# Selective scan of a two-layer conditioned network: new slot tables for the work laid around the scan, and SiLU work regrouped

## The chip, the core and the metric

One Trainium2 chip, one of its cores. The metric is device time of one launch in microseconds (us). A core has a matrix engine (TensorE, PE in the profile; its weight loads are PEld), VectorE (DVE), ScalarE (ACT), GpSimd (POOL) and SyncE (SP), which only issues transfers here. Each runs its own instruction stream in program order, and they wait for one another by semaphores.

## The reference, cut to what matters

Eight samples of 512 tokens by 512 features pass through a conditioned linear-attention layer, then through a layer with softmax attention and a selective scan. The change touches the scan and what follows it:

```python
# xm: layer-normed, scaled and shifted x, (b, 512, 512); DI = 1024, N = 16, K = 4
xr, z = split(xm @ W_in, 2)
u = silu(causal_conv(xr, W_conv, K) + b_conv)          # per channel, 4 taps
dt, Bm, Cm = split(u @ W_x, [64, 80])
delta = softplus(dt @ W_dt + b_dt)
A = -exp(A_log)
h = exp(delta_t * A) * h + (delta_t * u_t) * B_t       # for each t, 1024 x 16 states
y = sum(h * C_t) + u * D_param
ssm = (y * silu(z)) @ W_out
full = silu(ln(concat(ssm, attention)) @ W_full + b_full)
out = x + gate * full
```

Everything is float32.

## The kernel before

A setup block and a block with both attentions for all samples come first and are not touched. The last block, `mix` (L873), does the scan layer, and all that follows is about it.

**Units and slots.** A sample b is done in two halves (channels 0 to 511, then 512 to 1023); a half is 16 states times two groups of 256 channels, so 32 units. Each engine's stream has one step, called a slot, for each unit, and 32 slots make a half. In slot s

- ACT writes the decays exp(delta*A) of unit s+2 into one of two PSUM pairs (`decay`, L1187, two instructions). It must wait until the unit two before it is scanned (L1184);
- POOL writes delta*u*B of unit s+4 into one of six buffers (`dbu`, L1110), after PE has turned what lay in that buffer (L1105);
- DVE scans unit s+2 (L1342, one instruction over two times 512 steps) and then, from slot 2 on, adds two token tiles of y to `acc` (L1347, called the adds here);
- PE transposes two token tiles of a scanned state into `y_bank` (`turn`, L1480, eight matmuls, called the turn). Its two banks come free with DVE's adds of the slot before.

At slot 0 the half before is closed: PE turns `acc` back (`total`, L1489), DVE adds u*D and multiplies with silu(z) (L1356, L1360, L1367). Then PE turns four tiles of state 0, and ACT begins the new sum with them at its slot 1 (`set_sum`, L1218).

**Work laid into the slots.** After its scan work each engine does in a slot what dictionaries name for that slot (L925 to L960): `PE_XR = {0: 0, 1: 1, 3: 2, ...}` means that PE computes product xr2 in slot 3. Two streams of such work are laid beside a sample's scan:

- `front(n, s)`, beside half 1 of sample n-1: the products xr0 to xr7 (each four float32 matmuls, eight instructions in the profile, L1463), their convolution (first tap on ACT, `ACT_CONV0`, L1245, three taps on DVE, `DVE_CONV`, L1379), SiLU of u (`ACT_SILU_U`), the products z0 to z7, the projection xd, dt and C. Then softplus of channels 0 to 511: five ACT instructions for each 128 channels (`ACT_A1`), a pair of logarithms between two table loads (`ACT_LN1`), and four instructions on POOL (`POOL_CORR1`, `POOL_DELTA1`; L1116, L1119, L1125, L1128). The other four dt are done beside half 0 of sample n itself (`PE_DT0`, `ACT_A0`, `ACT_LN0`, `POOL_CORR0`, `POOL_DELTA0`).
- `tail(p, s)`, beside half 0 of sample p+1 and the first slots of its half 1 (counted on as slots 32, 33, ...): for each of four token tiles t the output product (`PE_O`, two slots), its copy (`ACT_O`), layer norm (`DVE_STATS`, `ACT_LN`, `DVE_NEWTON`, `ACT_NORM`), two transposes (`PE_CT`), their copies (`ACT_CT`), the last product (`PE_F`, two slots), the bias (`DVE_F`, L1416), SiLU (`ACT_OUT`), gate and residual on POOL (`POOL_OUT`, L1141, L1144) and the store (`SP_STORE`).

In half 1 PE does `front(n, 0)`, which holds xr0, ahead of slot 0's `total`. The first sample's `front` runs alone before the first scan, and the last sample's `tail` alone after the last.

**The ring.** All these products share two PSUM banks in program order (`Ring`, L73, and `order`, L976): a use waits until the use two before it was emptied (`wait_free`, L94), by ACT or DVE as named in `front_uses` and `tail_uses`. If the emptying sits in slot s+1 of ACT and the new use in slot s of PE, PE waits for an instruction that stands one slot later.

**ACT's tables.** SiLU is in another table set than the exponential. Each group of SiLU on ACT is led by an ACT_TABLE_LOAD and followed by one that brings the exponential back (`preload_act_table_set`). A sample has nine such groups: two for u, four for z (L1223, L1224) and three for the output (L1289, L1290). The logarithms of softplus add four groups.

**SyncE** issues the rows of B ahead of POOL (`load_row`, four rows, which are eight slots, ahead), the weights (`weights`, L1022: W_in, W_out and W_full take turns in two places), the attention tiles, x1 tiles, the gate and the stores, in its own slots.

Of the kernel before, what the change touches and what calls it, by code (L numbers as in the profile page):

```python
# [872 lines left out]
def mix(nc, a, out, space, bank, ident, col, aneg, convw, x1_d, xm_d, attn_d, gate_d, b_d, wide, load_wide, arrived):  # L873
    ctx = ExitStack()
    with ctx:
# [126 lines left out]
        with nc.Block() as block:  # L1002
# [174 lines left out]
            def _(act):  # L1177
# [48 lines left out]
                def front(n, s):  # L1226
                    if s in ACT_UD and n:
                        for c in ACT_UD[s]:
                            if n >= 2:
                                act.wait_ge(ring.full, ring.at(n - 2, "f3"))  # L1230
# [394 lines left out]
```

## Time and profile before

| | us |
|---|---|
| median of 3 runs (4289.5 to 4292.44) | 4291.6 |
| the profiled execution: its time | 4291.85 |
| the profiled execution: its span | 4290.1 |
| setup and attention, up to the `mix` block | about 1805 |
| `mix` | about 2485 |
| one sample in the middle of `mix` (two halves) | 296.97 |

In the timeline an instruction is printed with its start, its length, and in brackets how long its engine had been idle before it and which instruction ended that idle time. Neighbouring instructions of the same kind are merged (x2). The samples of `mix` repeat one another closely, so the sample that starts at 2757.93 (b = 3, whose half 1 starts at 2902.63) is read for all. A slot is counted from the start of its scan on DVE.

### The profile page before, as it was taken

The page shows a single profiled execution, that of the slowest core. Times are in us where ns is not written, and L with a number is a line of the kernel's source. Part 1 is how long each engine was busy: PE and PEld are TensorE (multiplying, and loading weights), DVE is VectorE, ACT ScalarE, POOL GpSimd, SP SyncE. Part 2 cuts the span into 40 slices and gives each one's busy share as a digit, 9 for nine tenths or more (in the row PEclk, how much of TensorE's full clock was granted, in tenths as well). Part 3 has the DMA queues.
Part 4 walks back from the last instruction along what each step waited for, and adds up shares of the span by engine and source line. Part 5 has one row for each costly group of instructions (what it writes and reads, how often), then busy time and mean ns, then how long its engine had stood idle before and what let it go on. Part 6 is the DMA issues. An engine that isn't in the chain of part 4 may idle for free.

```text
span 4290.1 us, 36188 instructions
## 1 busy us (share of the span) xinstructions
PE 3455.3 (81%) x12298; PEld 1819.9 (42%) x12298; DVE 2852.3 (66%) x3658; ACT 1991.9 (46%) x3326; POOL 1901.0 (44%) x1139
## 2 busy tenths in 40 slices
PE   5798989898898988676877787778787778878857
PEld 1444444343444443234444444444444444444444
DVE  1344445353535352349998888898889989888993
ACT  0232323232223231165666665675766657656743
POOL 0021212121212121147675775774766766757761
PEclk8899999999999999885888888889788888888858
DMA  5001010101010101011112222112121121122110
GB/s 201 32 1 42 0 42 1 42 1 42 1 42 1 42 1 69 29 33 35 60 66 81 71 78 85 62 66 80 64 79 65 64 79 64 69 87 71 43 51 20
DMA packets 99798, 220.85 MB, mean 51 GB/s; under 512 B 10576, under 2 KB 10688, under 8 KB 97568
## 3 DMA queue, kind: packets, MB, share of 16 engines
q1 hardware_dynamic: 95904, 211.06, 14.6%
q10 hardware_dynamic: 3712, 7.47, 0.5%
q8 instruction: 100, 1.64, 0.2%
q14 instruction: 82, 0.67, 0.0%
HBM read 184.67 MB, written 33.83 MB: 51 GB/s over the span
## 4 chain that ended last, share of the span: by engine, by line
PE 16%; DVE 16%; issue 9%; POOL 9%; ACT 7%; DMA 0%; POOLq 0%; SPq 0%; DVEq 0%
PE bank L1463 12%; DVE HS L1342 7%; DVE acc L1347 6%; POOL HS L1110 5%; PE bank L1480 4%; ACT bank L1187 2%; ACT G L1283 1%; POOL delta L1125 1%; POOL ZS L1116 1%; POOL DU L1128 1%; DVE U L1379 1%; PE bank L1489 1%; DVE G L1367 0%; ACT L1224 0%; DVE stats L1401 0%
## 5 line engine op out<-in xcount | busy, mean ns | idle before, releaser
L1110 POOL TENSOR_TENSOR HS<-DU,brep 128x1024 f32<-128x1024 f32 x512 | 1196.4, 2355 | 693.2 <-PE bank L1480 693.2
L1342 DVE TENSOR_TENSOR_SCAN HS<-bank,HS 128x1024 f32<-128x1024 f32 x512 | 1167.1, 2280 | 79.6 <-ACT bank L1187 59.4
L1480 PE MATMUL bank<-ident,HS 128*128 128x128 f32 x4096 | 697.8, 322 | 385.5 <-DVE acc L1347 351.0
L1187 ACT ACTIVATE bank<-delta,aneg 128x511 f32<-128x511 f32 x1024 | 662.9, 681 | 537.8 <-DVE HS L1342 536.2
L1480 PEld LDWEIGHTS bank<-ident,HS 128*128 128x128 f32 x4096 | 563.5, 165 | 660.1 <-DVE HS L1342 426.8
L1347 DVE SCALAR_TENSOR_TENSOR acc<-bank,C,acc 128x512 f32<-128x512 f32 x960 | 668.3, 737 | 146.0 <-PE bank L1480 144.9
L431 POOL TENSOR_TENSOR PR<-PR,rrec 128x512 f32<-128x512 f32 x256 | 261.3, 1042 | 895.2 <-DVE rrec L665 895.2
L1463 PE MATMUL bank<-w_l,G 128*128 128x512 f32 x1024 | 528.1, 666 | 42.2 <-ACT G L1283 40.2
L1463 PE MATMUL bank<-XM,w_l 128*128 128x512 f32 x1024 | 512.8, 649 | 30.3 <-ACT delta L1197 14.3
L520 ACT ACTIVATE PR<-bank,nsmax 128x512 f32<-128x512 f32 x256 | 173.5, 682 | 449.5 <-DVE nsmax L661 449.4
L715 PE MATMUL bank<-w_l,NT 128*128 128x512 f32 x768 | 358.5, 612 | 0.9 <-ACT NT L487 0.9
L1463 PEld LDWEIGHTS bank<-w_l,G 128*128 128x128 f32 x1024 | 213.1, 219 | 277.2 <-issue 232.1
L1463 PEld LDWEIGHTS bank<-XM,w_l 128*128 128x128 f32 x1024 | 207.2, 212 | 262.9 <-issue 222.7
L661 DVE TENSOR_REDUCE nsmax<-bank 128x1 f32<-128x512 f32 x256 | 164.7, 685 | 191.6 <-PE bank L815 191.6
L822 PE MATMUL bank<-ident,PR 128*128 128x128 f32 x1024 | 172.2, 294 | 134.5 <-DVE PT L672 121.4
L672 DVE COPY PT<-bank 128x512 f32<-128x512 f32 x256 | 175.4, 685 | 95.7 <-PE bank L822 95.7
L822 PEld LDWEIGHTS bank<-ident,PR 128*128 128x128 f32 x1024 | 121.6, 148 | 265.5 <-issue 225.8
L715 PE MATMUL bank<-XM,w_l 128*128 128x512 f32 x512 | 223.5, 597 | 6.8 <-issue 6.8
L715 PEld LDWEIGHTS bank<-w_l,NT 128*128 128x128 f32 x768 | 143.9, 197 | 171.1 <-issue 147.1
L1379 DVE SCALAR_TENSOR_TENSOR U<-bank,convw,U 128x509 f32<-128x509 f32 (+2 forms) x192 | 143.3, 747 | 52.7 <-ACT U L1245 48.2
L815 PE MATMUL bank<-K,Q 64*128 64x512 f32 x512 | 146.7, 650 | 9.4 <-ACT K L510 6.2
L715 PEld LDWEIGHTS bank<-XM,w_l 128*128 128x128 f32 x512 | 97.3, 191 | 132.5 <-issue 132.5
(164 smaller groups left out, 3817.8 us busy)
## 6 DMA issues: line engine op xcount, KB each, us to landing
brep<-b_d SPq DMA_DIRECT2D x256, 256.0 KB, 3.2
w_l<-in_L_cond_W_in SPq DMA_DIRECT2D x14, 2048.0 KB, 9.8
w_l<-in_L_cond_W_out SPq DMA_DIRECT2D x7, 2048.0 KB, 8.5
...
```

The lines of the kernel that those rows point to most:

```text
L431: nc.gpsimd.tensor_tensor(p, p, rrec[:, hp % 2, t, e:e + 1].to_broadcast([P, T]), ALU.mult).then_inc(pnorm, 1)
L520: nc.scalar.activation(PR[:, hp % 2, e, t, :], sc_bank[e][:], ACT.Exp, bias=nsmax[:, hp % 2, t, e:e + 1], accum_out=rsum[:, hp % 2, t, e:e ...
L672: nc.vector.tensor_copy(PT[:, k % 2, e, :], pt_bank[:]).then_inc(pt_done, 1)
L715: last = nc.tensor.matmul(dst[:], lhs(c), rhs(c), start=(c == 0), stop=(c == DC - 1))
L822: last = nc.tensor.transpose(pt_bank[:, t * P:(t + 1) * P], PR[:, hp % 2, e, t, k * P:(k + 1) * P], ident[:])
L1110: nc.gpsimd.tensor_tensor(HS[:, u % DEEP], DU[:, chunks(j, s), :], brep[:, m % 3, :].unsqueeze(1).to_broadcast([P, UC, T]), ALU.mult).then ...
L1187: last = nc.scalar.activation(dA[:, s, i, 1:T], delta[:, c, 1:T], ACT.Exp, scale=aneg[:, c, n:n + 1])
L1342: nc.vector.tensor_tensor_scan(h, dA[:, u % 2].rearrange("p i t -> p (i t)"), h, 0.0, ALU.mult, ALU.add).then_inc(scanned, 1)
L1347: nc.vector.scalar_tensor_tensor(out=acc[:, t, :], in0=y_bank[t % 2][:], scalar=C[:, j // 2 % 2, t, n:n + 1], in1=acc[:, t, :], op0=ALU.mu ...
L1379: last = nc.vector.scalar_tensor_tensor(out=y, in0=ring.bank(n, f"xr{c}")[:, 0:T - lag], scalar=convw[:, c, k:k + 1], in1=y, op0=ALU.mult, ...
L1463: last = nc.tensor.matmul(dst, lhs(c), rhs(c), start=(c == 0), stop=(c == of - 1))
L1480: last = nc.tensor.transpose(y_bank[t % 2][:, i * P:(i + 1) * P], h, ident[:])
```

## The change

It replaces the slot tables of `mix` and moves three pieces of ACT's work. Nothing is computed otherwise, and no instruction is added except through the order; ACT_TABLE_LOADs fall away.

- The eight xr products go from pairs (0, 1, 3, 4, 6, 7, 9, 10) to threes (0, 1, 2, 4, 5, 6, 8, 9), with the convolutions, z, xd, dt and C one to two slots earlier. The first tap of xr0 (`ACT_CONV0`) goes from slot 2 to slot 0, ahead of `set_sum`.
- SiLU of z goes from four groups of two to two groups of four, in slots 3 and 16 of half 0 of the sample itself (before: in slots 27 and 30 of half 1 before it, and 29 and 30 of half 0). SiLU of the output goes from three groups to one, at slot 36, and with it the POOL work and the stores of all four tiles to slots 37 to 41. That makes five groups in place of nine.
- Softplus of channels 0 to 511 goes from slots 20 to 25 to slots 17 to 24, with slot 19 left free.
- In `tail` the products go one or two slots forward, F0 goes ahead of O2, F1 ahead of O3, and the last F product ends in slot 30 rather than 31, its copy `ACT_CT` in slot 30 rather than 32.
- The u*D instructions of ACT get a function of their own, `skip`, with the same wait as before.

```diff
-        PE_XR = {0: 0, 1: 1, 3: 2, 4: 3, 6: 4, 7: 5, 9: 6, 10: 7}
-        PE_Z = {12: 0, 13: 1, 16: 2, 22: 3, 23: 4, 25: 5, 26: 6, 28: 7}
-        PE_XD = {14: 0, 15: 1}
-        PE_DT1, PE_C = {17: 0, 18: 1, 20: 2, 21: 3}, 19
-        PE_DT0 = {4: 4, 5: 5, 9: 6, 12: 7}
-        PE_O = {2: (0, 0), 3: (0, 1), 7: (1, 0), 8: (1, 1), 13: (2, 0), 14: (2, 1), 19: (3, 0), 20: (3, 1)}
-        PE_CT = {10: (0, 0), 11: (0, 1), 17: (1, 0), 18: (1, 1), 23: (2, 0), 24: (2, 1), 28: (3, 0), 29: (3, 1)}
-        PE_F = {15: (0, 0), 16: (0, 1), 21: (1, 0), 22: (1, 1), 26: (2, 0), 27: (2, 1), 30: (3, 0), 31: (3, 1)}
-        ACT_CONV0 = {2: 0, 3: 1, 5: 2, 6: 3, 8: 4, 9: 5, 11: 6, 12: 7}
-        ACT_UD = {4: (4, 5), 7: (6, 7)}
-        ACT_SILU_U = {9: (0, 1, 2, 3), 14: (4, 5, 6, 7)}
-        ACT_Z = {15: 0, 16: 1, 19: 2, 25: 3, 26: 4, 28: 5, 29: 6, 31: 7}
-        ACT_A1, ACT_LN1 = {20: 0, 21: 1, 23: 2, 24: 3}, {22: (0, 1), 25: (2, 3)}
-        ACT_A0, ACT_LN0 = {7: 4, 8: 5, 12: 6, 15: 7}, {9: (4, 5), 16: (6, 7)}
-        ACT_SILU_Z1, ACT_SILU_Z0 = {27: (0, 1), 30: (2, 3)}, {29: (4, 5), 30: (6, 7)}
-        ACT_O = {6: 0, 11: 1, 17: 2, 23: 3}
-        ACT_CT = {13: (0, 0), 14: (0, 1), 20: (1, 0), 21: (1, 1), 26: (2, 0), 27: (2, 1), 31: (3, 0), 32: (3, 1)}
-        ACT_OUT = {22: (0,), 28: (1,), 36: (2, 3)}
-        DVE_CONV = {1: 0, 2: 1, 4: 2, 5: 3, 7: 4, 8: 5, 10: 6, 11: 7}
-        DVE_STATS = {6: 0, 11: 1, 17: 2, 23: 3}
-        DVE_NEWTON = {8: 0, 13: 1, 19: 2, 25: 3}
-        DVE_F = {17: 0, 23: 1, 28: 2, 33: 3}
-        POOL_CORR1, POOL_DELTA1 = {22: 0, 24: 1, 26: 2, 28: 3}, {23: 0, 25: 1, 27: 2, 28: 3}
-        POOL_OUT = {23: 0, 29: 1, 37: 2, 38: 3}
-        SP_STORE = {25: 0, 31: 1, 39: 2, 40: 3}
+        PE_XR = {0: 0, 1: 1, 2: 2, 4: 3, 5: 4, 6: 5, 8: 6, 9: 7}
+        PE_Z = {10: 0, 11: 1, 14: 2, 20: 3, 22: 4, 23: 5, 25: 6, 26: 7}
+        PE_XD = {12: 0, 13: 1}
+        PE_DT1, PE_C = {15: 0, 16: 1, 18: 2, 19: 3}, 17
+        PE_DT0 = {3: 4, 4: 5, 7: 6, 9: 7}
+        PE_O = {1: (0, 0), 2: (0, 1), 5: (1, 0), 6: (1, 1), 14: (2, 0), 15: (2, 1), 20: (3, 0), 21: (3, 1)}
+        PE_CT = {10: (0, 0), 11: (0, 1), 16: (1, 0), 17: (1, 1), 22: (2, 0), 23: (2, 1), 27: (3, 0), 28: (3, 1)}
+        PE_F = {12: (0, 0), 13: (0, 1), 18: (1, 0), 19: (1, 1), 24: (2, 0), 25: (2, 1), 29: (3, 0), 30: (3, 1)}
+        ACT_CONV0 = {0: 0, 3: 1, 4: 2, 6: 3, 7: 4, 8: 5, 10: 6, 11: 7}
+        ACT_UD = {6: (4, 5), 7: (6, 7)}
+        ACT_SILU_U = {9: (0, 1, 2, 3), 13: (4, 5, 6, 7)}
+        ACT_Z = {12: 0, 14: 1, 16: 2, 23: 3, 25: 4, 26: 5, 28: 6, 29: 7}
+        ACT_A1, ACT_LN1 = {17: 0, 18: 1, 21: 2, 22: 3}, {20: (0, 1), 24: (2, 3)}
+        ACT_A0, ACT_LN0 = {6: 4, 7: 5, 10: 6, 11: 7}, {8: (4, 5), 14: (6, 7)}
+        ACT_SILU_Z = {3: (0, 1, 2, 3), 16: (4, 5, 6, 7)}
+        ACT_O = {5: 0, 9: 1, 18: 2, 24: 3}
+        ACT_CT = {12: (0, 0), 13: (0, 1), 18: (1, 0), 19: (1, 1), 24: (2, 0), 25: (2, 1), 29: (3, 0), 30: (3, 1)}
+        ACT_OUT = {36: (0, 1, 2, 3)}
+        DVE_CONV = {1: 0, 2: 1, 3: 2, 5: 3, 6: 4, 7: 5, 9: 6, 10: 7}
+        DVE_STATS = {4: 0, 8: 1, 17: 2, 23: 3}
+        DVE_NEWTON = {6: 0, 10: 1, 19: 2, 25: 3}
+        DVE_F = {14: 0, 20: 1, 26: 2, 31: 3}
+        POOL_CORR1, POOL_DELTA1 = {20: 0, 22: 1, 24: 2, 26: 3}, {21: 0, 23: 1, 25: 2, 27: 3}
+        POOL_OUT = {37: 0, 38: 1, 39: 2, 40: 3}
+        SP_STORE = {38: 0, 39: 1, 40: 2, 41: 3}
...
+                def skip(b, s):
+                    if s in ACT_UD:
+                        for c in ACT_UD[s]:
+                            if b:
+                                act.wait_ge(ring.full, ring.at(b - 1, "f3"))
+                            nc.scalar.activation(G[:, c, :], U[:, c, :], ACT.Identity, scale=col("L1_cond_D_param", c)).then_inc(ud_done, 1)
...
-                    if s in ACT_SILU_Z1:
-                        silu_z(n, ACT_SILU_Z1[s])
...
-                        if s in ACT_SILU_Z0:
-                            silu_z(b, ACT_SILU_Z0[s])
+                        if s in ACT_SILU_Z:
+                            silu_z(b, ACT_SILU_Z[s])
```

`DVE_XD`, `DVE_C`, `ACT_LN`, `ACT_NORM`, `POOL_CORR0`, `POOL_DELTA0` and SP's slots for B, x1, attention and gate move by up to three slots in the same way.

## Rows read from the trace of the kernel before

**Rows 1.** The page, parts 1 and 4: busy time, and shares of the chain.
```profile
PE 3455.3 (81%) x12298; PEld 1819.9 (42%) x12298; DVE 2852.3 (66%) x3658; ACT 1991.9 (46%) x3326; POOL 1901.0 (44%) x1139
...
PE 16%; DVE 16%; issue 9%; POOL 9%; ACT 7%; DMA 0%; POOLq 0%; SPq 0%; DVEq 0%
```
**Rows 2.** Windows: stretch, its length, then PE, PEld, DVE, ACT, POOL busy, granted clock.
```profile
2757.93:3054.90 296.97, 231.82 (x868) 131.67 (x868) 260.70 (x268) 192.55 (x299) 199.02 (x105) 0.85 0.22 72
...
2842.00:2848.60 6.60, 5.82 (x7) 2.52 (x8) 5.74 (x8) 4.95 (x11) 6.38 (x5) 0.50 0.22 82
```
**Rows 3.** Waits of DVE in 2757.93 to 3054.9: total, times, longest.
```profile
DVE acc L1347 <- PE bank L1480: 20.5, 14, 6.1
DVE bank L1356 <- PE bank L1489: 4.3, 2, 4.1
DVE HS L1342 <- ACT bank L1187: 3.4, 2, 3.3
DVE U L1379 <- ACT U L1245: 3.2, 1, 3.2
DVE HS L1342 <- POOL HS L1110: 2.7, 1, 2.7
```
**Rows 4.** Timeline, half 0: a plain slot, then slots 13 to 15, and 20.
```profile
2774.47 1.22 PE L1480 MATMUL bank<-ident,HS 128*128 128x128 f32 x8 [0.16 <-DVE acc L1347]
2774.89 2.28 DVE L1342 TENSOR_TENSOR_SCAN HS<-bank,HS 128x1024 f32<-128x1024 f32 x1
...
2778.40 2.28 DVE L1342 TENSOR_TENSOR_SCAN HS<-bank,HS 128x1024 f32<-128x1024 f32 x1
...
2816.29 4.45 PE L1463 MATMUL bank<-w_l,G 128*128 128x512 f32 x8
...
2821.45 3.60 PE L1463 MATMUL bank<-w_l,G 128*128 128x512 f32 x8
2824.88 1.04 PE L1480 MATMUL bank<-ident,HS 128*128 128x128 f32 x8
2825.76 3.60 PE L1463 MATMUL bank<-w_l,G 128*128 128x512 f32 x8
...
2825.52 1.41 DVE L1347 SCALAR_TENSOR_TENSOR acc<-bank,C,acc 128x512 f32<-128x512 f32 x2 [0.70 <-PE bank L1480]
...
2849.89 1.41 DVE L1347 SCALAR_TENSOR_TENSOR acc<-bank,C,acc 128x512 f32<-128x512 f32 x2 [2.05 <-PE bank L1480]
```
**Rows 5.** Timeline where half 0 ends and half 1 begins.
```profile
2894.44 6.39 PE L1463 MATMUL bank<-w_l,G 128*128 128x512 f32 x8 [4.36 <-ACT G L1283]
...
2904.97 3.60 PE L1463 MATMUL bank<-XM,w_l 128*128 128x512 f32 x8
...
2909.04 1.41 DVE L1356 SCALAR_TENSOR_TENSOR bank<-U,cols,bank 128x512 f32<-128x512 f32 x2 [4.14 <-PE bank L1489]
...
2917.10 1.26 ACT L1218 ACTIVATE acc<-bank,C 128x512 f32<-128x512 f32 x2 [0.47 <-PE bank L1480]
```
**Rows 6.** Timeline, late slots of half 1.
```profile
3016.21 5.26 PE L1463 MATMUL bank<-XM,w_l 128*128 128x512 f32 x8 [1.51 <-ACT delta L1197]
...
3021.94 1.41 DVE L1347 SCALAR_TENSOR_TENSOR acc<-bank,C,acc 128x512 f32<-128x512 f32 x2 [4.26 <-PE bank L1480]
...
3011.92 1.27 POOL L1119 TENSOR_TENSOR DU<-DU,ZS 128x512 f32<-128x512 f32 x1 [3.98 <-ACT DU L1210]
3013.15 2.35 POOL L1110 TENSOR_TENSOR HS<-DU,brep 128x1024 f32<-128x1024 f32 x1
...
3018.03 2.35 POOL L1110 TENSOR_TENSOR HS<-DU,brep 128x1024 f32<-128x1024 f32 x1
```
**Rows 7.** A group of 2757.93 to 3054.9: busy, mean ns, idle; and ACT's largest wait.
```profile
L1223 ACT ACT_TABLE_LOAD x4 | 5.1, 1283 | 0.1
...
ACT bank L1187 <- DVE HS L1342: 63.2, 32, 4.4
```
**Rows 8.** Timeline, POOL's last instruction.
```profile
4286.29 1.26 POOL L1144 TENSOR_TENSOR comb<-comb 128x512 f32<-128x512 f32 x1
```

More of the change, by code:

```diff
@@ L940, in mix @@
-        ACT_SILU_Z1, ACT_SILU_Z0 = {27: (0, 1), 30: (2, 3)}, {29: (4, 5), 30: (6, 7)}
-        ACT_O = {6: 0, 11: 1, 17: 2, 23: 3}
-        ACT_LN = {8: 0, 13: 1, 19: 2, 25: 3}
-        ACT_NORM = {10: 0, 15: 1, 21: 2, 27: 3}
-        ACT_CT = {13: (0, 0), 14: (0, 1), 20: (1, 0), 21: (1, 1), 26: (2, 0), 27: (2, 1), 31: (3, 0), 32: (3, 1)}
-        ACT_OUT = {22: (0,), 28: (1,), 36: (2, 3)}
-        DVE_CONV = {1: 0, 2: 1, 4: 2, 5: 3, 7: 4, 8: 5, 10: 6, 11: 7}
-        DVE_XD, DVE_C = 16, 20
-        DVE_STATS = {6: 0, 11: 1, 17: 2, 23: 3}
@@ L950, in mix @@
-        DVE_NEWTON = {8: 0, 13: 1, 19: 2, 25: 3}
-        DVE_F = {17: 0, 23: 1, 28: 2, 33: 3}
-        POOL_CORR1, POOL_DELTA1 = {22: 0, 24: 1, 26: 2, 28: 3}, {23: 0, 25: 1, 27: 2, 28: 3}
-        POOL_CORR0, POOL_DELTA0 = {10: 4, 12: 5, 17: 6, 19: 7}, {11: 4, 13: 5, 18: 6, 20: 7}
-        POOL_OUT = {23: 0, 29: 1, 37: 2, 38: 3}
-        SP_B, SP_OUT, SP_ATTN, SP_GATE, SP_XM = 18, 13, {10: 0, 12: 1, 14: 2, 16: 3}, 8, 1
-        SP_X1 = {13: 0, 20: 1, 26: 2, 31: 3}
-        SP_STORE = {25: 0, 31: 1, 39: 2, 40: 3}
+        PE_XR = {0: 0, 1: 1, 2: 2, 4: 3, 5: 4, 6: 5, 8: 6, 9: 7}
@@ new lines, in mix @@
+        ACT_LN = {7: 0, 11: 1, 20: 2, 26: 3}
+        ACT_NORM = {9: 0, 13: 1, 22: 2, 27: 3}
+        ACT_CT = {12: (0, 0), 13: (0, 1), 18: (1, 0), 19: (1, 1), 24: (2, 0), 25: (2, 1), 29: (3, 0), 30: (3, 1)}
+        ACT_OUT = {36: (0, 1, 2, 3)}
+        DVE_CONV = {1: 0, 2: 1, 3: 2, 5: 3, 6: 4, 7: 5, 9: 6, 10: 7}
+        DVE_XD, DVE_C = 14, 18
+        DVE_STATS = {4: 0, 8: 1, 17: 2, 23: 3}
+        DVE_NEWTON = {6: 0, 10: 1, 19: 2, 25: 3}
+        DVE_F = {14: 0, 20: 1, 26: 2, 31: 3}
+        POOL_CORR1, POOL_DELTA1 = {20: 0, 22: 1, 24: 2, 26: 3}, {21: 0, 23: 1, 25: 2, 27: 3}
@@ L960, in mix @@
+        POOL_CORR0, POOL_DELTA0 = {9: 4, 11: 5, 15: 6, 17: 7}, {10: 4, 12: 5, 16: 6, 18: 7}
+        POOL_OUT = {37: 0, 38: 1, 39: 2, 40: 3}
+        SP_B, SP_OUT, SP_ATTN, SP_GATE, SP_XM = 16, 13, {11: 0, 12: 1, 14: 2, 16: 3}, 10, 1
+        SP_X1 = {13: 0, 19: 1, 25: 2, 30: 3}
+        SP_STORE = {38: 0, 39: 1, 40: 2, 41: 3}
         SP_XR, SP_Z = 24, 2
@@ L1224, in silu_z @@
                     act.preload_act_table_set(EXP_AND_LN)
-                def front(n, s):
[L1227 to L1230, printed above, removed]
-                            nc.scalar.activation(G[:, c, :], U[:, c, :], ACT.Identity, scale=col("L1_cond_D_param", c)).then_inc(ud_done, 1)
+                def skip(b, s):
[4 more added lines that the diff above has]
+                            nc.scalar.activation(G[:, c, :], U[:, c, :], ACT.Identity, scale=col("L1_cond_D_param", c)).then_inc(ud_done, 1)
+                def front(n, s):
                     if s in ACT_SILU_U:
@@ L1312, in half1 @@
                             tail(p, s + SLOTS)
+                        skip(b, s)
                         if n is not None:
                             front(n, s)
-                        elif s in ACT_UD:
-                            front(b + 1, s)
                 act.preload_act_table_set(EXP_AND_LN)
```

## The prediction

> **What bounds the kernel now.** I read the page first. No engine is full over the whole launch, and the chain of the end is shared by PE and DVE [rows 1]: such a view only says that stages must be looked at one by one. The windows come next. A sample of `mix` takes 296.97 us, of which DVE works 260.70 and every other engine less [rows 2]. DVE's work is the same after the change, so DVE's 36.3 us of idle time in a sample are all that can be won: 7 x 36.3 = 254 us at the very most. The waits of DVE say whom it waits for [rows 3]: 20.5 us in the adds for PE's turn, 4.3 at the closing of a half, 3.4 and 2.7 for decays and for POOL, 3.2 for the first tap. The 14 waits of the adds are one of 6.1, one of 4.3, one of 2.05, eight of 0.70 and three that make up the other 2.5 [rows 3, 4, 6].
>
> Last the timeline, for why a turn is late. A plain slot is 3.50 us, and the adds are due when the scan ends, 2.28 after it began. A free turn ends 0.80 after the scan's start [rows 4]. A product at 2.4 GHz holds PE for 3.43, then the adds begin 0.64 after the next turn began, and product slots follow at 4.31 [rows 4]. So a lone product is ready at about 0.7 + 3.43 + 0.64 = 4.8 where 5.8 is due: free, with 1.0 to spare. Each further slot in a row costs 0.81. **A run of n products stalls DVE by 0.81n - 1.8**, plus what its first product loses at the lower clock (6.39 against 3.60, so 2.8 [rows 5]; 0.85 if only in part [rows 4]), plus its late start, minus DVE's own extra work within the run.
>
> **The change part by part**, for one sample, as the stall that goes and the one that comes.
>
> (1) The end of half 0. F3's first part stood in slot 30 and waited 4.36 for an ACT copy of slot 31, ran 6.39 at 1.2 GHz, and F3's second part and xr0 then both stood between the last turn and `total` [rows 5]. DVE lost 6.1 and 4.1, with 0.17 for a decay 10.4. Now the copies stand in the same slots 29 and 30 as the products, and ACT runs over a slot ahead of PE, as its decay must. Only xr0 is left ahead of `total`. A run of three, first product at the low clock: 0.81 x 3 - 1.8 + 2.8 = 3.4, less 0.2, since the turn before `total` has a little more room: 3.2. **-7.2** (bounds: 0.6 with no low clock, -9.8; 6.6 with two such products, -3.8).
>
> (2) The first tap. ACT did it after `set_sum`, whose last two instructions begin at 2917.10 [rows 5], and DVE waited 3.2. In slot 0 it is done before; it waits there only for DVE's first u*D. Next is the decay for slot 2, behind `set_sum`: 2917.10 + 1.26 + 1.3 = 2919.6, where DVE, done with its scan and three taps (2.3, which fill what was idle), would be ready 0.8 earlier. So 0.8 stays: **-2.4**. The one group of SiLU for four output tiles stands in ACT's slot 4 ahead of the third tap (2 x 1.28 + 4 x 0.62 = 5.0): +0.3 (0 to 2.5, its whole overhang).
>
> (3) The runs of slots 13 to 16 and 19 to 22 cost 2.6 and 4.15 (2.05 and three of 0.70). They become 12 to 15 and 18 to 21. O3 no longer waits for an ACT copy one slot later, which was 0.9, and F's bias (0.68) and the Newton step (0.87) now fall within the runs. First run 1.4 + 2.0 low clock - 0.7 - 0.3 = 2.4; second 1.4 + 2.5 - 1.0 (it follows a slot made long by the statistics) - 0.9 - 0.6 = 1.4. **-3.0** (-5 if the array is fast, +1 if both first products are wholly slow). F2: +0.3.
>
> (4) O0 now stands in slot 1, ahead of the turn for slot 2's adds, where it had none in front before, and O1 in slots 5 and 6 has little DVE work beside it: 0.3 + 0.8 + 0.3 = **+1.4** (0 to 5: a wholly slow O0a is 2.8 more).
>
> (5) z0, z1, xd, xd, z2 in half 1 stalled 2.4, with xd waiting for z0's copy one slot later. That is now in its own slot, and z0 lies beside a convolution, so four products count: 1.4 - 0.5 + 0.3: **-1.2** (-2.4 to +1). SiLU of u in slot 13 is now in the slot of the xd that needs it; it was one slot ahead.
>
> (6) Late in half 1. z3 waited 1.51 for softplus's Relu in ACT's next slot and took 5.26, partly at 1.2 GHz; DVE lost 4.3 + 0.7 [rows 6]. POOL had waited 3.98 for the logarithm [rows 6] and then put an extra pair of instructions after each product: 4.88 for each slot [rows 6] against DVE's 3.50, until DVE waited 2.7 [rows 3]. The sum is 7.7. Eased by slot 19, the logarithm ends 5.5 after slot 18's scan began. POOL then needs 1.3 + 7 x 4.88 + 2.35 = 37.8 more to the end of the product for slot 29, which is 43.3, where 11 slots give it 38.5: DVE loses 4.8 in all, and z3's stall, still about 2.9 since it again waits for ACT's next slot, lies within them. **-2.9** (-4 to +1). POOL is what is late next here.
>
> (7) Eight table loads fall away, 8 x 1.28 = 10.3 us of ACT [rows 7]. I count nothing: ACT waits 63.2 us for DVE's scans in a sample [rows 7], which covers them; without that cover they would be worth up to 10.3. The Trainium skill, page "ScalarE: Activation LUTs", section "What ACT_TABLE_LOAD costs", says that a switch costs about 2.66 with a drain; by that ACT would gain 21.3 in a sample, and with the same cover the sum would be the same. The row's 1283 ns agrees with the page's load alone.
>
> (8) POOL's output work moves to slots 5 to 8 of half 1, where convolutions make DVE's slots about 5.7 long: 2.35 + 2 x 1.26 = 4.9 fits. SP's stores go behind it, and rows of B and weights queue behind the stores; rows are issued eight slots (28 us) ahead. Nothing, and 2 to 3 us for each wait if that lead were gone.
>
> Sum: -7.2 - 2.4 + 0.3 - 3.0 + 0.3 + 1.4 - 1.2 - 2.9 = **-14.7 for a sample**, 7 times (the first sample has no `tail` beside it, the last no `front`): -103. At the start two SiLU groups go, 4 x 1.28 = 5.1 and more on ACT, but POOL's first product, 1892.96 + 2.35, stands only 2.2 before the end of the first decay, 1896.27 + 1.25 [rows 8]: -2 (0 to -5). At the end the output work of all four tiles is left for after the last copies: POOL does 4 x 2.7 in a row where the last pair ended at 4287.55 [rows 8], about +5 (+2 to +9). 4291.85 - 103 - 2 + 5 = 4192 for the profiled execution, which lies 0.25 above the median of the runs: **4192 us**.
>
> **The rivals.** *ACT's lead is not there (0.22).* Groups of four hold a decay up for 5.0 rather than 3.7, in slot 3 after `set_sum` has used up ACT's lead, in slot 13 against xd, and in slot 36 against a tap. At 2.5 to 3 each that is 8 in a sample: 4192 + 56 = 4248. For it: ACT's copies waited on in rows 5 and 6. Against: the 63.2 of idle time.
>
> *The stalls move less than I think, or more (0.06 and 0.07).* Should POOL and z3 add rather than overlap, 2.9 a sample, 4212, is inside the forecast. Should most first products be fast, 4160 or a little less.
>
> *The array is cold (0.06), slower.* The granted clock was 0.50 in a stretch that began with O3 after two light slots, and 0.85 over the sample [rows 2]. The change ends z two slots earlier and leaves other light stretches. A product inside a run that becomes wholly slow costs 2.8. To lose the 100 us and 9 more takes 109 / 7 / 2.8 = 5.6 more of the sample's 34 in that state; with seven, 4192 + 7 x 7 x 2.8 = 4329. The Trainium skill, "TensorE: Matmul & The Clock Gate", section "HAM oscillation — how this bites in real kernels", says that idle gaps throw the array back to the half rate again and again; by it the threes would each start slow, which rows 2 and 5 bear out for the runs of today.
>
> *It does not do what it says (0.03).* The tables could only shift work from one stall to another and leave 36 us of idle time: 4292.
>
> **How the numbers follow.** Forecast, 4160 to 4228: 0.56; ACT's lead, 4228 to 4270: 0.22; larger gain, 4130 to 4160: 0.07; smaller gains by other causes, to 4283: 0.06; no change 0.03; slower 0.06. The range 4158 to 4252 holds the forecast, most of the first rival and the bounds of (1) and (3) together. Faster by over 0.2% (below 4283), about what a measurement of this kernel tells from no change: 0.91; within it 0.03; slower 0.06.
>
> **What would show it.** In a sample of the changed kernel: a period near 282 with DVE still at 260.7; the waits for PE's turn down from 20.5 to about 14, with the one of 6.1 gone; the closing of half 0 near 1 instead of 4.1; no wait of the taps above 1; POOL's wait before a scan late in half 1 of 2 to 5. I am wrong if decays make DVE wait more than 6 in a sample (ACT's lead), or if the granted clock falls well below 0.85.

## The result, and the profile after

| | median us | runs |
|---|---|---|
| before | 4292.02 | 4 (4289.5 to 4292.49) |
| after | 4128.31 | 4 (4126.34 to 4129.32) |

The ratio is 0.9619, with a 95% interval of 0.9602 to 0.9636. The change gains 163.7 us where 100 was forecast, and the time lies 30 us below the range. The profiled execution took 4128.04 us, with a span of 4126.2. Counted from the scans on DVE, the first scan starts 1.1 us earlier; sample 0, whose half 1 alone changes, is 7.6 shorter; each of the next six periods goes from 296.97 to 272.95, 24.0 shorter, together 144.2; the last half with a `tail` beside it is 12.3 shorter, and what follows the last scan 1.4 longer. Together that is 163.8, the difference of the two profiled executions. In the comparisons further down, 5 of 34 executions of the kernel before took 13 to 23 us less than their median, and one of four of `sum_o0` took 15 less; no trace of one was kept.

The page, parts 1 and 4, of the changed kernel, beside [rows 1]:

```profile
PE 3383.7 (82%) x12298; PEld 1802.2 (44%) x12298; DVE 2844.3 (69%) x3658; ACT 1906.8 (46%) x3262; POOL 1901.7 (46%) x1139
...
POOL 17%; issue 13%; PE 13%; DVE 10%; ACT 3%; DMA 0%; POOLq 0%; SPq 0%; DVEq 0%
```

DVE does the same 3658 instructions in 8 us less; the rest of the gain is idle time. POOL now has the largest share of the chain, 17% for 9%.

The same sample, b = 3, in the windows (PE, PEld, DVE, ACT, POOL busy, granted clock), with one stretch at the low clock under it, beside [rows 2]:

```profile
2700.41:2973.49 273.08, 223.49 (x868) 130.59 (x868) 259.56 (x268) 181.83 (x291) 199.10 (x105) 0.87 0.24 79
2739.29:2749.49 10.20, 6.73 (x22) 4.49 (x22) 10.12 (x13) 10.07 (x19) 9.53 (x7) 0.50 0.08 27
```

The clock is hardly higher, 0.87 for 0.85. But look at the second row: in a low stretch DVE is busy for 10.12 of 10.20 us. That stretch has only transposes and a short dt product in it, and there the low clock costs DVE nothing. The waits of DVE in this sample, beside [rows 3]:

```profile
DVE acc L1345 <- PE bank L1478: 5.8, 5, 3.7
DVE HS L1340 <- ACT bank L1187: 3.7, 2, 3.3
DVE HS L1340 <- POOL HS L1110: 1.6, 2, 1.3
DVE bank L1358 <- PE bank L1487: 0.8, 2, 0.6
DVE bank L1354 <- PE bank L1487: 0.2, 1, 0.2
```

The adds wait 5.8 us for PE instead of 20.5; the forecast had 14. The waits at the closing of 4.1 and of the tap of 3.2 are gone. What is left for ACT is one wait of 3.26 at the start of half 0, which the kernel before has too, and one of 0.42 in half 1.

The timeline of the end of half 0 (F3's two parts, xr0, the closing's transposes, then `total`, the scan and the adds), beside [rows 5], and then the places of F0 and z3, beside [rows 4, 6]:

```profile
2822.34 3.60 PE L1461 MATMUL bank<-w_l,G 128*128 128x512 f32 x8
2826.64 3.60 PE L1461 MATMUL bank<-w_l,G 128*128 128x512 f32 x8
2830.95 3.60 PE L1461 MATMUL bank<-XM,w_l 128*128 128x512 f32 x8
2834.39 1.04 PE L1487 MATMUL bank<-ident,acc 128*128 128x128 f32 x8
2835.03 1.42 DVE L1354 SCALAR_TENSOR_TENSOR bank<-U,cols,bank 128x512 f32<-128x512 f32 x2
2845.21 2.29 DVE L1340 TENSOR_TENSOR_SCAN HS<-bank,HS 128x1024 f32<-128x1024 f32 x1 [0.42 <-ACT bank L1187]
2848.15 1.41 DVE L1345 SCALAR_TENSOR_TENSOR acc<-bank,C,acc 128x512 f32<-128x512 f32 x2 [0.65 <-PE bank L1478]
...
2741.13 1.94 PE L1478 MATMUL bank<-ident,HS 128*128 128x128 f32 x8 [2.27 <-DVE acc L1345]
2755.19 3.60 PE L1461 MATMUL bank<-w_l,G 128*128 128x512 f32 x8
...
2924.40 1.26 POOL L1119 TENSOR_TENSOR DU<-DU,ZS 128x512 f32<-128x512 f32 x1 [2.35 <-ACT DU L1210]
2928.69 6.25 PE L1461 MATMUL bank<-XM,w_l 128*128 128x512 f32 x8 [1.02 <-ACT delta L1197]
2935.41 1.41 DVE L1345 SCALAR_TENSOR_TENSOR acc<-bank,C,acc 128x512 f32<-128x512 f32 x2 [3.75 <-PE bank L1478]
2962.98 2.29 DVE L1340 TENSOR_TENSOR_SCAN HS<-bank,HS 128x1024 f32<-128x1024 f32 x1 [1.30 <-POOL HS L1110]
```

F3's first part takes 3.60 here where it took 6.39, and `total` at 2835.03 has no bracket: nothing is waited for. F0a, the head of a run of four, takes 3.60 as well. The low clock meets transposes ahead of them, four slots ahead of F0 and one slot ahead of F3 (1.94 for the 1.04 to 1.22 at the full clock), and these have room. The heads F1a and F2a are slow in part, 4.67 and 4.48. z3 alone is as slow as the slow heads of before, 6.25, in a stretch from 2920.19 to 2933.89.

### The profile page after: what moved, and what is told of

Its sections match the earlier page's. It is cut to its first block, busy times and chain, and to the rows that moved or that the text cites. A ratio compares the mean times of both kernels' runs of the same rounds, so it can differ in the third digit from the quotient of the medians.

```text
span 4126.2 us, 36124 instructions
## 1 busy us (share of the span) xinstructions
PE 3383.7 (82%) x12298; PEld 1802.2 (44%) x12298; DVE 2844.3 (69%) x3658; ACT 1906.8 (46%) x3262; POOL 1901.7 (46%) x1139
## 4 chain that ended last, share of the span: by engine, by line
POOL 17%; issue 13%; PE 13%; DVE 10%; ACT 3%; DMA 0%; POOLq 0%; SPq 0%; DVEq 0%
POOL HS L1110 12%; PE bank L1461 10%; DVE HS L1340 5%; DVE acc L1345 4%; PE bank L1478 3%; POOL delta L1125 1%; POOL DU L1128 1%; POOL ZS L1116 1%; ACT bank L1187 1%; DVE U L1377 1%; POOL comb L1141 1%; POOL DU L1119 0%; PE bank L1487 0%; POOL comb L1144 0%; DVE G L1365 0%
## 5 line engine op out<-in xcount | busy, mean ns | idle before, releaser
L1461 PE MATMUL bank<-XM,w_l 128*128 128x512 f32 x1024 | 502.4, 638 | 43.8 <-DVE U L1377 18.9
L1461 PE MATMUL bank<-w_l,G 128*128 128x512 f32 x1024 | 473.5, 608 | 9.4 <-ACT delta L1197 3.9
L1461 PEld LDWEIGHTS bank<-w_l,G 128*128 128x128 f32 x1024 | 192.8, 198 | 209.0 <-issue 200.6
L715 PE MATMUL bank<-XM,w_l 128*128 128x512 f32 x512 | 223.4, 597 | 6.8 <-issue 6.8
```

The lines of the kernel that those rows point to most:

```text
L715: last = nc.tensor.matmul(dst[:], lhs(c), rhs(c), start=(c == 0), stop=(c == DC - 1))
L1461: last = nc.tensor.matmul(dst, lhs(c), rhs(c), start=(c == 0), stop=(c == of - 1))
```

## The experiments

All times are medians of 4 runs (10 for `before_warm18`), the kernel before is at 4289.8 to 4292.0 in each comparison, and idle times are those of DVE in sample b = 3, where no other sample is named.

### Which half's tables bring it

`tail_only` is the kernel before with the half-0 tables of the change (the products, transposes, copies, statistics and Newton steps of `tail`, dt0 and its softplus). `front_only` is the kernel before with the half-1 tables (xr, z, xd, dt1, C, convolutions, their softplus). Both keep the nine groups of SiLU.

```diff
 tail_only:
-        PE_F = {15: (0, 0), ... 30: (3, 0), 31: (3, 1)}
+        PE_F = {12: (0, 0), ... 29: (3, 0), 30: (3, 1)}
 front_only:
-        PE_XR = {0: 0, 1: 1, 3: 2, 4: 3, ...}
+        PE_XR = {0: 0, 1: 1, 2: 2, 4: 3, ...}
```

> The kernel before with only the tables of half 0 of the change (O, CT, F, their copies, statistics, dt and softplus of channels 512 to 1023); front and SiLU groups as before. By the prediction's terms (1), (3), (4), with the low clock at the first products as I had put it: 8.5 us a sample, 4292 - 7 x 8.5 = 4232. By the theory that the tables also move the low clock away from the first products, half 0 and the closing shorten as in the changed kernel, 144.7 to 132.4 and 4.1 at the closing: 16.4 a sample, 4177. By the theory that the removed table loads carry the gain: near 4292, since none is removed.

> The kernel before with only the tables of half 1 of the change (xr in threes, first tap in slot 0, z, xd, softplus of channels 0 to 511); tail and SiLU groups as before. By the prediction's terms (2), (5), (6) 6.5 us a sample, 4247; by what half 1 lost in the changed kernel without the closing, 152.2 to 140.7 less 4.1, 7.4 a sample, 4240. If the two halves of the change help each other (the clock carried from one to the other), less than that: 4250 or more.

Measured: 4218.03 (ratio 0.9839, 0.981 to 0.9868) and 4219.67 (0.9843, 0.9819 to 0.9868). Against the 4290.84 of the kernel before in this comparison, the half-0 tables bring 73 us and the half-1 tables 71. `tail_only` was expected at 4232, or at 4177 if the tables alone kept the low clock off the heads. It took neither: the closing's 4.14 is 0.61 and F3a takes 3.60, but with the two SiLU groups still in slots 29 and 30 a decay there is 2.91 late, and in half 1 the first tap waits 4.02 for 3.16. `front_only` brings 27 more than the 4247 of the terms. Of its 10.2 us a sample, 7.1 are where the tables changed: the tap 3.16 to 0.95 with the adds behind it, the run with z0 and xd 2.43 to 0.16, z3 and POOL 7.6 to 5.3. The other 3.1 fell in half 0, whose tables are untouched: the wait of 2.05 at slot 20 is 0.20, and that of 6.11 is 4.69. The place is on PE. O3a took 4.78 instead of 6.63 and F3a 5.46 instead of 6.39: the stretch at O3a began about 3 us ahead of its slot's scan and no longer just behind it, and that at F3a lasted about 7 us where it was 10.5. So a change in one half moves the low stretches of the other.

### The SiLU groups

`nine_groups` is the changed kernel with SiLU of z and of the output in nine groups as before (the output's one slot earlier, as the tail is). `z_groups` puts only those of z back.

```diff
-        ACT_SILU_Z = {3: (0, 1, 2, 3), 16: (4, 5, 6, 7)}
+        ACT_SILU_Z1, ACT_SILU_Z0 = {27: (0, 1), 30: (2, 3)}, {29: (4, 5), 30: (6, 7)}
 nine_groups alone:
-        ACT_OUT = {36: (0, 1, 2, 3)}
+        ACT_OUT = {21: (0,), 27: (1,), 36: (2, 3)}
```

> The changed kernel with nine groups of SiLU on ACT again: z in slots 27 and 30 of half 1 and 29 and 30 of half 0, the output in slots 21, 27 and 36, POOL and the stores behind them. By the prediction's term (7), ACT's idle time covers the loads: 4128, within 5. By the rival that ACT's table loads are on the path: 8 x 1.28 x 7 = 72 more, 4200.

> The changed kernel with the SiLU of z in its four old groups (slots 27 and 30 of half 1, 29 and 30 of half 0), the output still in one group. Theory: it is the two groups that stand beside the copies of F3 in slots 29 and 30 of half 0 that cost 22 us in the kernel with nine groups; the groups of the output cost nothing. Then 4150 us, with a wait of about 2.6 us for a decay at slot 30 of half 0. Rival, the output groups in slots 21 and 27 share the cost: 4135 to 4142 us.

Measured: 4150.32 (0.968, 0.9656 to 0.9704) and 4155.05 (0.9689, 0.9669 to 0.9709), so term (7) as it stood is refuted, and so is the full 72. The z groups alone cost all of it, 22 to 27 us; the groups of the output cost nothing. The timeline of `z_groups`, ACT and the scan that waits:

```profile
2837.57 1.28 ACT L1223 ACT_TABLE_LOAD   x1
2838.86 1.15 ACT L1223 ACTIVATE ZS<-ZS 128x512 f32<-128x512 f32 x2
2840.03 1.28 ACT L1224 ACT_TABLE_LOAD   x1
2841.33 2.52 ACT L1187 ACTIVATE bank<-delta,aneg 128x511 f32<-128x511 f32 x4
2842.66 2.29 DVE L1342 TENSOR_TENSOR_SCAN HS<-bank,HS 128x1024 f32<-128x1024 f32 x1 [2.56 <-ACT bank L1187]
```

A group of two costs ACT 3.7 us, of which 2.56 are the two loads. Two groups stand in slots 29 and 30, with a copy of F3 (1.48) each, and the decay is 2.56 late. The closing and the decay of the first tap's place add 0.5 and 0.6, the adds behind it give 0.3 back: DVE waits 3.1 to 3.3 more in a sample, 7 x 3.2 = 22. The loads are 1.28 each, and what follows starts 0.01 later. The Trainium skill, "ScalarE: Activation LUTs", section "What ACT_TABLE_LOAD costs", puts a switch at about 2.66 with a drain; this trace shows the load and no drain, and the measured number decides.

### The end of half 0

`f3_late` is the changed kernel with F3, its copies and its bias in the slots of before.

```diff
-        PE_F  ... 29: (3, 0), 30: (3, 1)      ACT_CT ... 29: (3, 0), 30: (3, 1)
+        PE_F  ... 30: (3, 0), 31: (3, 1)      ACT_CT ... 31: (3, 0), 32: (3, 1)
```

> The changed kernel with F3 in slots 30 and 31 again, its copies in ACT's slots 31 and 32 and its bias in slot 33. The closing must cost DVE 3.5 to 4.3 us a sample again, since F3's second part and xr0 both stand between the last turn and total. Theory A, that the wait of 6.1 came from ACT's copies being late behind two SiLU groups in ACT's slots 29 and 30: these are gone here, ACT's copy is only some 1 us late, PE does not idle, the clock stays high, and the waits are 4 to 5.5 in all: 4128 + 7 x 5 = 4163. Theory B, that the slots alone set it: 10.4 a sample as before, 4200.

Measured: 4161.3 (0.9706, 0.9679 to 0.9733). The windows and the timeline of `f3_late`, sample b = 3 and behind it b = 4:

```profile
2712.27:2988.86 276.59, 223.96 (x868) 130.58 (x868) 259.49 (x268) 181.66 (x291) 199.02 (x105) 0.88 0.23 78
2838.81 4.22 PE L1461 MATMUL bank<-w_l,G 128*128 128x512 f32 x8 [0.23 <-ACT G L1282]
2847.18 3.60 PE L1461 MATMUL bank<-XM,w_l 128*128 128x512 f32 x8
2851.25 1.41 DVE L1354 SCALAR_TENSOR_TENSOR bank<-U,cols,bank 128x512 f32<-128x512 f32 x2 [4.14 <-PE bank L1487]
...
2988.86:3268.65 279.79, 227.99 (x868) 132.98 (x868) 259.69 (x267) 181.90 (x291) 199.09 (x105) 0.86 0.23 77
3115.35 5.89 PE L1461 MATMUL bank<-w_l,G 128*128 128x512 f32 x8 [0.23 <-ACT G L1282]
3121.71 1.41 DVE L1345 SCALAR_TENSOR_TENSOR acc<-bank,C,acc 128x512 f32<-128x512 f32 x2 [2.33 <-PE bank L1478]
```

The wait of 4.14 at the closing is back to the hundredth in both samples, as in [rows 5], with F3b and xr0 between the last turn and `total`. The wait of 6.1 is not back. Without the two SiLU groups the copy comes nearly in time (F3a waits 0.23 for it, where it waited 4.36), and the wait is 0.66 in b = 3, where F3a takes 4.22, and 2.33 in b = 4, where it takes 5.89. The samples of this launch go between the two, so that their mean period is 278.6. So the 10.4 of term (1) had more than one cause. The slots alone cost 4.8, with F3a mostly at the full clock (b = 3). A slow F3a adds 1.7 with the copy in time (b = 4, which runs the same instructions). The other 4 went with ACT's late copies. 4163 was expected from the copies' lateness, and 4161 came, but by two kinds of sample and not by one.

### The first tap

`conv0_slot2` is the changed kernel with `ACT_CONV0 = {2: 0, ...}`.

> The changed kernel with ACT's first tap of xr0 back in slot 2 of half 1. By term (2) of the prediction DVE waits 2.4 us more in each sample that has another behind it: 4128 + 17 = 4145 us. Rival: the tap in slot 0 was no gain, because the convolution only fills time that DVE else waits for the decay behind set_sum: 4128 to 4132 us.

Measured: 4152.56 (0.9684, 0.9664 to 0.9704), slower than the changed kernel by 24.

```profile
2857.30 2.31 DVE L1377 SCALAR_TENSOR_TENSOR U<-bank,convw,U 128x509 f32<-128x509 f32 x3 [3.51 <-ACT U L1246]
```

3.51 comes in place of 0.42 and 0.65: 2.44, as term (2) said. Another 0.5 is z3's stall (4.25 for 3.75, the product 6.76 for 6.25 at the low clock), and the periods alternate between 275.7 and 277.2, so that their mean is 3.4 above that of the changed kernel. In a sample of 277.2 (b = 4) z3 stalls 3.56, but F3a takes 4.52 and the adds behind F3 wait 0.52 and 0.70. The step is right; the sum left out what the clock does to other products.

### Late in half 1

Two changes to the changed kernel, alone and together. `z3_late` has z3 in slot 21, behind the Relu that it waited for. `pool_split` takes one of the two subtractions on POOL out of the crowded slots:

```diff
-        PE_Z = {... 20: 3, 22: 4, ...}
+        PE_Z = {... 21: 3, 22: 4, ...}
+        POOL_W1 = {18: 0, 19: 1, 22: 2, 23: 3}
+                    if s in POOL_W1:
+                        error(n, POOL_W1[s])      # w1 - e_abs, until now the first half of correct()
```

> The changed kernel with z3 in PE's slot 21, where its bank is emptied in ACT's slot 21, no longer one slot later. Theory of the prediction's term (6): the 3.75 for z3's turn fall to 1.5 or less, but POOL's backlog is the limit and its waits of 1.58 grow to what makes 5.3 in all, so the time stays: 4128, within 4. Rival, that z3's wait is added to POOL's: 2 to 3 us a sample less, 4110.

> The changed kernel with the first of softplus's four POOL instructions (w1 - e_abs, for channels 0 to 511) in slots of its own, 18, 19, 22 and 23, so that two of them leave POOL's crowded slots for idle ones. By the theory of POOL's backlog 2.5 us less work there: its waits of 1.58 go, z3's of 3.75 stays: 4128 - 7 x 1.6 = 4117. If POOL only waits for the logarithm of slot 20 a little longer instead: 4128.

> The changed kernel with both: z3 in slot 21 and the split POOL work. By the theory that z3 and POOL are two limits that lie within one another, only the two together bring 2.5 us a sample: 4128 - 7 x 2.5 = 4110. By the theory that each counts for itself: the sum of what the two runs before it show.

Measured: 4127.50, 4127.32 (both 0.9624, 0.9602 to 0.9647) and 4120.88 (0.961, 0.9587 to 0.9633). In `z3_late` the 3.75 became 1.06 and twice 0.70, and DVE's waits for POOL grew from 1.58 to 2.23. That is term (6)'s picture, in which z3's stall lies within POOL's backlog, but only in part, since the waits of the place still fell from 5.33 to 4.69. In `pool_split` POOL's waits are gone and z3's is 4.15, and yet the time is the same. The waits that came instead, 0.22 and 0.70 behind F0, 0.50 and 0.70 behind O0, are those of products at the low clock (F0a 4.22, O0a 4.47): it lies at slots 10 to 12 of half 0 there, and at 8 to 10 in the changed kernel. `z3_pool`, both together, beats both kernels: its four runs (4117.5 to 4123.8) lie below the four of the changed kernel (4126.3 to 4129.3), by 7.4 us in the median, where 18 were expected. Its windows for b = 2 and b = 3, then for b = 3 the timeline at the decay behind `set_sum`, at O1a, and behind z3:

```profile
2420.60:2691.18 270.58, 219.21 (x868) 127.65 (x868) 259.67 (x268) 181.68 (x291) 198.97 (x105) 0.89 0.24 79
2691.18:2964.32 273.14, 222.21 (x868) 129.61 (x868) 260.04 (x268) 181.68 (x291) 198.85 (x105) 0.88 0.23 79
...
2704.63 2.29 DVE L1347 TENSOR_TENSOR_SCAN HS<-bank,HS 128x1024 f32<-128x1024 f32 x1 [3.26 <-ACT bank L1194]
2707.66 1.41 DVE L1352 SCALAR_TENSOR_TENSOR acc<-bank,C,acc 128x512 f32<-128x512 f32 x2 [0.74 <-PE bank L1485]
...
2718.14 5.40 PE L1468 MATMUL bank<-w_l,G 128*128 128x512 f32 x8 [0.56 <-ACT delta L1204]
...
2929.20 1.41 DVE L1352 SCALAR_TENSOR_TENSOR acc<-bank,C,acc 128x512 f32<-128x512 f32 x2 [1.02 <-PE bank L1485]
```

Late in half 1 the two together did bring nearly the 2.5 expected, 5.33 down to 3.0. But in b = 3 to 5 the period is 273.05 to 273.14, as in the changed kernel: O0a and F0a take 4.71 and 4.33 in b = 3, and half 0 is 2.4 longer. In b = 2 of the same launch both take 3.60 and the period is 270.58. Of the 10.4 us between the two profiled executions, 3.8 lie ahead of the first scan, 1.8 in sample 0, 3.6 in b = 1 and 2, nothing in b = 3 to 5, and 1.2 behind them. So the same instructions take 2.5 us a sample more or less with the place of the low stretch, which is as much as the edit was worth.

### The low clock itself

In these two the kernel before is run with some turns done three times over (the same transposes into the same bank), which makes PE busier and changes nothing else. `before_busy` does it in 12 light slots of half 0 and 14 of half 1, `before_warm18` in slots 17 and 18 of half 0 only.

```diff
-                        for i in range(HC):
+                        for i in list(range(HC)) * times:
```

> The kernel before with the turn's transposes done three times over (the same data to the same place) in the slots that hold no product, so that TensorE is busier there and nothing else changes. By the theory that the low clock at the first product of a run is a cost of its own: granted clock up from 0.87, and the waits of 6.1, 2.05 and 0.5 in the adds shorter by 2.8, 2 and 0.5, with the z product of half 1 1.7 shorter: some 6 us a sample, 4292 - 45 = 4247. If the low clock is hidden by DVE's work: 4292, or up to 10 more for the longer turns.

> The kernel before, with the transposes of slots 17 and 18 of half 0 done three times, so that PE is busier just ahead of O3a, which took 6.63 us at the low clock in the profiled sample. Theory: a product at the low clock inside a run costs what the sum said; O3a becomes about 4.3 us or less, the wait of 2.05 us at slot 20 goes to about 0.7, and the time falls by 7 x 1.4 = 10 us, to 4282. Rival: the low stretch only moves to another run of products and is paid there, 4290 to 4300.

Measured: 4318.68 (1.0074, 1.0049 to 1.0098) and 4288.89 (1.0002, 0.9987 to 1.0016). The window of the sample and the waits for PE in `before_busy`:

```profile
2769.59:3066.71 297.12, 257.40 (x1284) 166.81 (x1284) 261.09 (x267) 192.67 (x299) 199.29 (x105) 0.94 0.22 72
...
DVE acc L1348 <- PE bank L1481: 23.0, 23, 5.4
```

With the clock at 0.94 instead of 0.85 PE's waits are 23.0, more than the 20.5 of before, and the period is the same, 297.12 for 296.97. Every other sample takes 300.2, at 0.93: there O3a meets the low clock (6.78) and the wait at slot 20 is 2.19, about what it was. Three such samples make 10 of the 26 us between the two profiled executions. The others lie mostly in the first half of scans and in the last, where no `tail` or `front` stands beside them: there the tripled turns bring waits for PE of 8.8 and 7.7 us that the kernel before doesn't have. In b = 3, where the array is fast, waits do shrink (2.05 to 0.60 at slot 20); the extra transposes make new ones (nine of 0.47 to 1.58), and the large ones stay: 5.37 for ACT's copy, 4.14 for the slots at the closing. A high mean clock is no aim by itself.

`before_warm18` is the sharper test. O3a fell from 6.63 to 4.59, its 2.05 is gone and the 6.11 is 4.68. But the period is 296.97, as in [rows 2], since other waits grew:

```profile
2813.65 5.28 PE L1464 MATMUL bank<-w_l,G 128*128 128x512 f32 x8
2819.40 1.41 DVE L1348 SCALAR_TENSOR_TENSOR acc<-bank,C,acc 128x512 f32<-128x512 f32 x2 [1.35 <-PE bank L1481]
...
2833.20 0.75 DVE L1348 SCALAR_TENSOR_TENSOR acc<-bank,C,acc 128x512 f32<-128x512 f32 x1 [1.58 <-PE bank L1481]
```

The low stretch lies at slots 11 to 14 now, over O2a, the head of the first run: 5.28 where it took 4.45 [rows 4], and 1.35 of waiting where it was 0.52. Slot 17 waits 1.58 and 0.56 for the tripled transposes themselves, where it was 0.70, and z3 waits 5.31 for 4.26. Half 0 is 0.7 shorter and half 1 0.7 longer. So what the fast O3a gave was paid in two ways: at other products that met a low stretch, as the rival said, and by 1.4 for the tripled turn itself, which the rival didn't have. The test doesn't part the two cleanly.

### The start of half 0

The largest wait left, 3.26, is for a decay behind `set_sum`. `sum_later` is `z3_pool` with `set_sum` one slot later on ACT, behind that decay; `sum_o0` has O0 in slots 2 and 3 instead of 1 and 2 as well; `o0_late` has only O0 moved.

```diff
-                        if s == 1:
+                        if s == 2:
                             set_sum(b * 2)          # in half 1 set_sum(b * 2 + 1) likewise
 sum_o0, o0_late:
-        PE_O = {1: (0, 0), 2: (0, 1), ...}
+        PE_O = {2: (0, 0), 3: (0, 1), ...}      # O0's copy, statistics, Newton step and norm one slot later too
```

> Kernel z3_pool (the product of z3 a slot later, the subtraction of the error of c = 0 to 3 on POOL), and set_sum on ACT one slot later, behind the decay of slot 4 that stood behind it. Theory: the wait of 3.26 us for that decay at the start of half 0 (and 0.6 + 0.4 in half 1) is due to this order alone and goes; nothing is late behind set_sum, since the next decay has until the adds of slot 2 are done. 4121 - 8 x 3.2 - 7 x 0.5 = 4092 us. Rival: the wait moves to the next decay or to the adds of slot 2, which need the turn behind set_sum: 4110 to 4121 us.

> Kernel sum_later (set_sum behind the next decay) with O0 in slots 2 and 3 as well. In sum_later O0a, 4.68 us at the low clock, stands on PE between the first turn and the one that the adds of slot 2 need, and DVE waits 4.08 us there. Theory: without it that wait is about 1.1 us (the turn begins when set_sum has freed the banks), and O0a then costs 2.4 us one slot later if it is at the low clock still, 1.3 if it is not, so that 0.3 to 1.5 us of a sample's 4.78 go: 4110 to 4118 us. Rival: set_sum's own length on ACT bounds the place, the waits stay near 4, 4120 us.

> Kernel z3_pool with the product O0 in slots 2 and 3 of half 0 instead of 1 and 2 (its copy, statistics, logarithm, Newton step and norm one slot later too). Term (4) of the prediction held that O0a in slot 1, ahead of the turn for slot 2's adds, costs 0.3 to 1.4 us in a sample. But the decay behind set_sum makes DVE wait 3.26 us in the same place, and O0a runs beside that wait. Theory: the product is hidden there, and in slots 2 and 3 the pair costs as much again, 4121 to 4128 us. Rival: term (4) as written, 4111 to 4118 us.

Measured: 4120.07 (0.9608, 0.9588 to 0.9629), 4123.18 (0.9603, 0.9586 to 0.9621) and 4131.84 (0.9629, 0.9613 to 0.9645). In `sum_later` the wait for the decay is gone and stands behind the next thing:

```profile
2710.04 4.68 PE L1468 MATMUL bank<-w_l,G 128*128 128x512 f32 x8
2715.20 1.41 DVE L1352 SCALAR_TENSOR_TENSOR acc<-bank,C,acc 128x512 f32<-128x512 f32 x2 [4.08 <-PE bank L1485]
```

O0a, at the low clock, stands between the first turn and the one that these adds need. In `sum_o0` it does not, and the 4.78 of the place become 3.0 (0.27, 0.93, 0.96, 0.85):

```profile
2716.68 1.41 DVE L1352 SCALAR_TENSOR_TENSOR acc<-bank,C,acc 128x512 f32<-128x512 f32 x2 [0.93 <-PE bank L1485]
...
2754.34 4.84 PE L1468 MATMUL bank<-w_l,G 128*128 128x512 f32 x8
...
2823.41 4.44 PE L1468 MATMUL bank<-w_l,G 128*128 128x512 f32 x8
...
2832.63 1.41 DVE L1352 SCALAR_TENSOR_TENSOR acc<-bank,C,acc 128x512 f32<-128x512 f32 x2 [0.70 <-PE bank L1485]
```

Locally that is the gain expected, and the time still doesn't fall: F0a (4.84) and F3a (4.44) now meet a low stretch, and 0.5 and 1.14 of waiting come back there. `o0_late` shows the same on its own: at O0 DVE waits 0.24 for 1.44, a gain of 1.2 that the theory of hiding didn't allow, and 0.57 behind F0 and 1.17 behind F3 are lost; the time is 11 us longer than that of `z3_pool`, and its periods go up and down between 271.5 and 275.9. Both expectations for it were wrong.

## Why the prediction was wrong

The direction and the list of places were right, and so were the rule for a run and most of the waits behind the terms; the price at the low clock was not, nor term (7), and the sum was 64 us short. Per sample, what was forecast to be left of each stall, and what the changed kernel's sample has:

| term | left, forecast | left, measured |
|---|---|---|
| (1) end of half 0 | 3.2 | 0.15 |
| (2) first tap, with SiLU's 0.3 | 1.1 | 1.07 |
| (3) run 12 to 15, run 18 to 21, F2 | 2.4, 1.4, 0.3 | 0.71, 0, 0 |
| (4) O0, O1 | 1.4 | 0.58 |
| (5) z0 to z2 | 1.2 | 0.16 |
| (6) z3 and POOL | 4.8 | 5.33 |
| untouched (start of half 0) | 4.0 | 4.0 |
| sum | 19.8 | 12.0 |

**The step that failed is the price of the first product of a run.** Terms (1) and (3) charged 2.8, 2.0 and 2.5 us for heads of runs at 1.2 GHz, and term (4) left 0.8 for part of one. Measured: F3a 0, F0a 0, F1a 1.07. Take those prices in place of mine and the same rule, 0.81n - 1.8, gives 0.4 for (1), 0.4 for the first run and nothing for the second (1.4 + 1.07 - 2.5), against 0.15, 0.71 and 0. The rule comes within about 0.3 of each, and the add-on is what was off. I had read the slow heads in the trace of before (4.45 in [rows 4], 6.39 in [rows 5]) as a property of a run after light slots. But the low stretch has its own place, and can as well lie over the transposes ahead: at 0.50 DVE is 99% busy there. These add-ons are 6.2 of the 7.8 us a sample (2.8 of (1), 2.0 and 1.4 of (3)). The period fell 9.3 more than forecast: the 7.8, 1.1 of DVE's own time, and 0.4 of rounding in the forecast's column. Six periods make 56 of the 64 us; the first sample's half 1 and the last one's half 0 make 5, and the end 4, less 1 at the start. In the prediction's own words this is the case in which most first products are fast, given 0.07 and 4160 or a little less; its size was too small, since I let it take only 4.6 a sample off, the full-clock bounds of (1) and (3).

What the rival of the cold array took from the Trainium skill, "TensorE: Matmul & The Clock Gate", section "HAM oscillation — how this bites in real kernels", is seen in half 1: the heads of two of the three xr runs took 4.85 and 4.62, and another xr product 4.62. Beside convolutions they cost at most the 0.65 of the adds above. But F0a and F3a, heads of runs too, took 3.60 after 2.71 and 0.71 us in which PE waited. So the rule shows in part of the trace and doesn't give the time here: what counts is whether a product without room lies in the slow stretch.

**Where the low stretches lie is not settled.** Small edits moved them by one or more slots, in parts of the sample that the edits don't touch (`front_only`, `before_warm18`, `pool_split`, `o0_late`), and each move gave or took 0.5 to 2 us at a product. In `z3_pool` and `f3_late` they lie in different places in different samples of one launch, with 2.5 and 3.2 us between the periods, and nothing differs in the instructions. The head of the first run of half 0 took 3.60, 4.22, 4.45, 4.84 and 5.28 in five kernels. So part of the 164 us, and all of any difference in this study under some 10 us, can belong to where the stretches happened to fall and not to the edit. That the changed kernel's heads are fast by its design was not shown: no experiment puts a low stretch over F0a or F3a of the changed kernel and leaves all else.

**Smaller errors.** (7) counted nothing for the loads and groups that leave ACT, because ACT waits 63.2 us in a sample. `z_groups` gives 22 to 27 us. The average was no cover in slots 29 and 30, where three things meet: two groups of SiLU, two copies and decays that are due every 3.5. The sum didn't suffer by it, since (1) took for granted that ACT would be in time there, but it put the gain down to the slots alone; `f3_late` shows that it had other causes too. DVE's busy time fell by 1.1 a sample, spread over adds and small instructions, where none was counted. At the start 2 was forecast and 1.1 came; the two starts that term is worked out from, 1892.96 and 1896.27, are in the trace of before but not in [rows 8]. At the end 5 was forecast and 1.4 came:

```profile
4113.45 1.26 POOL L1141 TENSOR_TENSOR comb<-comb,gate 128x512 f32<-128x512 f32 x1 [88.00 <-ACT comb L1288]
...
4122.48 1.26 POOL L1144 TENSOR_TENSOR comb<-comb 128x512 f32<-128x512 f32 x1
```

POOL's four pairs do take 10.3 us in a row, as said; but they begin at 4113.45, while PE is at F3's last product until 4117.2, since three of the four tiles don't wait for F3. I had put the whole row behind the last copies. POOL is done 1.4 later after the last scan than in the kernel before.

**What held.** ACT's lead did not fail: decays make DVE wait 3.7 us, of which 3.26 are old. (2) was 0.03 off and `conv0_slot2` confirms it. (5) ended 1.0 better, (6) 0.5 worse, and POOL is what is late next: with z3's stall mostly out of the way (`z3_late`) 0.6 of the place's 5.3 is gained, with both (`z3_pool`) 2.3. (8), SP's queue and the stores: no wait for them shows. The rival of a change that only shifts waits is refuted for this change (34.9 us of idle time a sample become 12.0), but it describes the later attempts at the start of half 0, and b = 3 of `z3_pool`.
